# Fetching four consecutive ranks' sums with one indirect transfer in the third layer's node stage

## The reference

```
q, k, v = x @ Wq + bq, x @ Wk + bk, x @ Wv + bv          # 8 heads of 16
e = edge_attr @ We
alpha = softmax over the edges of one node of (q[dst] * (k[src] + e)).sum / 4
agg   = segment_sum(alpha * (v[src] + e), dst)            # 50,000 x 128, zero where a node has no edge
h     = layernorm(agg + x @ Wskip + bskip + x)
x     = layernorm(x + layernorm(gelu(h @ Wf1 + bf1) @ Wf2 + bf2 + h))
```

## Time and profile before

| | |
|---|---|
| Time, median of 3 runs | 7075.83 us (7072.01 to 7086.69) |
| The profiled execution's own time | 7071.4 us |
| Its span, first to last instruction | 7069.7 us |
| Mean granted TensorE clock | 0.883 of full speed |
| Busy over the span: PE, DVE, ACT, POOL | 75%, 59%, 39%, 60% |
| `nodes_2`, from POOL's first fetch to its last scatter | 4332 to 5837 us |
| Busy in 4458 to 5720 us (1262 us): PE, DVE, ACT, POOL | 850.7, 603.9, 655.0, 646.1 us |
| Indirect transfers L435 in the stage | 392, mean 969 ns of POOL |

### The profile page before, as it was taken

One profiled execution on the slowest core, in us unless ns is written; L12 is line 12 of the kernel. 1 busy time (PEld: TensorE's weight loads), 2 busy tenths in 40 slices (PEclk: granted clock), 3 DMA queues, 4 the chain that ended last, 5 costly groups with the idle time before them and its releaser, 6 DMA issues. The chain is left out here.

```text
span 7069.7 us, 108538 instructions
## 1 busy us (share of the span) xinstructions
PE 5276.6 (75%) x29030; PEld 3736.3 (53%) x29030; DVE 4158.6 (59%) x14866; ACT 2748.0 (39%) x6645; POOL 4214.4 (60%) x3907
## 2 busy tenths in 40 slices
PE   4776889788866665787699996766666675776788
PEld 3655677545455554333488874333333344555566
DVE  4454777523345555777488884544445454655698
ACT  0000555411111212666355554555555462222354
POOL 4664466666668886777644442455555445554598
PEclk9898999988888887999799998888888887888899
DMA  4554666444456666999545552333333332333466
GB/s 128 174 173 150 178 179 177 136 124 135 131 117 107 106 108 128 317 301 303 176 141 147 152 148 74 90 86 88 86 89 90 84 87 60 74 72 72 121 185 175
DMA packets 1163875, 966.37 MB, mean 137 GB/s; under 512 B 161046, under 2 KB 975586, under 8 KB 1163268
## 3 DMA queue, kind: packets, MB, share of 16 engines
q1 hardware_dynamic: 977956, 684.36, 32.2%
q0 software_dynamic: 163072, 210.16, 15.4%
q10 hardware_dynamic: 22240, 64.90, 2.5%
HBM read 485.30 MB, written 496.79 MB: 139 GB/s over the span
## 5 line engine op out<-in xcount | busy, mean ns | idle before, releaser
L2337 PE MATMUL l_nodes_f<-l_nodes_h_t_s,w_f 128*128 128x512 f32 x784 | 435.7, 684 | 433.4 <-ACT l_nodes_act_t L2289 422.9
L526 POOL DMA_INDIRECT tgt_tab<-l_nodes_ext,rank_at x392 | 389.9, 995 | 580.9 <-ACT l_nodes_ext L2312 474.0
L1556 POOL DMA_INDIRECT agg<-l_edges_b_rows,l_edges_b_at x392 | 608.5, 1552 | 133.9 <-issue 79.4
L1844 POOL DMA_INDIRECT l_edges_kv<-kv_tab,src_i x392 | 397.7, 1015 | 400.6 <-DVE l_edges_v_e L1865 291.2
L526 POOL DMA_INDIRECT to_col<-l_nodes_col_s,rank_row x392 | 415.4, 1060 | 326.6 <-ACT l_nodes_col_s L1250 232.3
L2510 POOL DMA_INDIRECT l_edges_proj<-proj_tab,src_i x392 | 382.3, 975 | 376.8 <-DVE l_edges_msg L2483 247.7
L435 POOL DMA_INDIRECT l_nodes_ag<-agg,sum_at x392 | 380.0, 969 | 241.4 <-issue 119.5
L961 POOL DMA_INDIRECT l_edges_fetched<-in_x,src_i x392 | 381.5, 973 | 218.8 <-DMA dst_i<-in_dst 111.0
L1314 POOL DMA_INDIRECT l_edges_a_at_row<-to_row,src_i x392 | 378.2, 965 | 219.0 <-issue 111.6
L526 POOL DMA_INDIRECT q_tab<-l_nodes_qkvs,rank_at x392 | 403.0, 1028 | 149.5 <-issue 105.9
L891 ACT COPY l_edges_rows<-l_edges_sums 128x264 f32<-128x264 f32 (+1 forms) x294 | 122.1, 450 | 947.9 <-DMA dst_i<-in_dst 463.7
(11 more groups left out here) (359 smaller groups left out, 14716.8 us busy)
## 6 DMA issues: line engine op xcount, KB each, us to landing
agg<-zeros ACTq DMA_DIRECT2D x98, 516.0 KB
l_nodes_xg<-x SPq DMA_DIRECT2D x196, 256.0 KB
kv_tab<-l_nodes_qkvs SPq DMA_DIRECT2D x98, 512.0 KB
agg<-l_edges_rows SPq DMA_DIRECT2D x98, 266.0 KB
l_nodes_ag<-agg SPq DMA_DIRECT2D x98, 266.0 KB
proj_tab<-l_nodes_ext SPq DMA_DIRECT2D x98, 264.0 KB
l_nodes_ag<-agg SPq DMA_DIRECT2D x98, 258.0 KB
l_nodes_ag_odd<-agg SPq DMA_DIRECT2D x98, 258.0 KB
```

Source lines behind the costliest of these rows:

```text
L526: pool.indirect_dma_start(table, bass.IndirectOffsetOnAxis(ranks[:, n * G + j:n * G + j + 1].bitcast(U32), 0), rows[:, j, :], None, bounds ...
L1556: pool.indirect_dma_start(agg1[j // 2], bass.IndirectOffsetOnAxis(at[k][:, j:j + 1].bitcast(U32), 0), rows[k][:, j, :], None, compute_op=A ...
L1844: pool.indirect_dma_start(kv[k][:, j, :], None, kv_tab, bass.IndirectOffsetOnAxis(src_i[:, n * G + j:n * G + j + 1].bitcast(U32), 0),).the ...
L2337: pe.matmul(f[m % 2][:], w_f1[:, m * P:(m + 1) * P], h_t_s[k][:], start=True, stop=True).then_inc(f_done, 1)
```

## The change

The four transfers of a group become one. It reads, for each partition, a run of four consecutive rows of `agg2` (512 floats, 2 KB) that begins at the lowest of the partition's four row numbers. Since the four nodes' ranks ascend, the row of each of them is one of the four in the run. A node without edges has the row number `held`; it takes nothing from the run, or zeros where `held` lies in it. Marks decide it.

`rank_rows` for the nodes now leaves, in place of `sum_at`, the tile `run_at` (128 x 98, the lowest row number for each partition and group) and `run_mark` (128 x 98 x 4 x 4 floats): mark m, j is 1 where node j's row is row m of the run and 0 elsewhere. Marks with j below m are neither written nor used, since row m of a run can't belong to an earlier node than the m-th.

In `conv` DVE now computes, instead of one addition, `ua[j] = skip[j] + sum over m of ag[m] * mark[m, j]`: 4 + 3 + 2 + 1 = 10 operations on 128 x 128, each a multiplication by a value per partition and an addition. An operation with m above 0 waits through the new semaphore `chosen` for the one that wrote the same part of `ua`.

```diff
-        sum_at, rank_at = (sb0(n, [P, tiles], I32) for n in ("sum_at", "rank_at"))
+        rank_at, run_at = sb0("rank_at", [P, tiles], I32), sb0("run_at", [P, groups], I32)
+        run_mark = sb0("run_mark", [P, groups, G, G])
...
-        def sum_fetcher(space, table, width):
+        def run_fetcher(space, table, width):
...
-            a_in = [[sem(f"a_in{k}{j}") for j in range(G)] for k in range(RING)]
+            a_in = [sem(f"a_in{k}") for k in range(RING)]
...
-                for j in range(G):
-                    pool.indirect_dma_start(
-                        ag[k][:, j, :], None, table, bass.IndirectOffsetOnAxis(sum_at[:, n * G + j:n * G + j + 1].bitcast(U32), 0),
-                    ).then_inc(a_in[k][j], 16)
+                pool.indirect_dma_start(
+                    ag[k][:].rearrange("p j d -> p (j d)"), None, table, bass.IndirectOffsetOnAxis(run_at[:, n:n + 1].bitcast(U32), 0),
+                ).then_inc(a_in[k], 16)
...
-                for j in range(G):
-                    eng.wait_ge(a_in[k][j], i * 16 + 16)
+                eng.wait_ge(a_in[k], i * 16 + 16)
...
-                            for m, (at_p, to) in enumerate(((whole_p, rows), (opens_p, rank_at))):
-                                dve.wait_ge(turned, m + 1)
-                                chain(dve.tensor_copy(to[:].rearrange("p (g j) -> p j g", j=G),
-                                                      at_p[:, 0:tiles].rearrange("p (j g) -> p j g", j=G)))
+                            by_run = "p (j g) -> p g j"
+                            dve.wait_ge(turned, 1)
+                            chain(dve.tensor_copy(sum_f[:], whole_p[:, 0:tiles].rearrange(by_run, j=G)))
+                            chain(dve.tensor_reduce(base[:], sum_f[:], AX.X, ALU.min))
+                            chain(dve.tensor_copy(rows[:], base[:]))
+                            chain(dve.tensor_tensor(sum_f[:], sum_f[:], by_group, ALU.subtract))
+                            for m in range(G):
+                                chain(dve.tensor_scalar(run_mark[:, :, m, m:], sum_f[:, :, m:], float(m), None, ALU.is_equal))
+                            dve.wait_ge(turned, 2)
+                            chain(dve.tensor_copy(rank_at[:].rearrange("p (g j) -> p g j", j=G), opens_p[:, 0:tiles].rearrange(by_run, j=G)))
...
-                            dve.tensor_tensor(ua[k][:], ag[k][:], skip[k][:], ALU.add).then_inc(ua_done, 1)
-                            dve.wait_ge(ua_done, n + 1)
+                            done = n * (G * (G + 1) // 2)
+                            for m in range(G):
+                                for j in range(m, G):
+                                    if m:
+                                        dve.wait_ge(chosen, done - (G - m) + 1)
+                                    so_far = ua[k] if m else skip[k]
+                                    last = dve.scalar_tensor_tensor(ua[k][:, j, :], ag[k][:, m, :], run_mark[:, n, m, j:j + 1], so_far[:, j, :],
+                                                                    ALU.mult, ALU.add).then_inc(chosen, 1)
+                                    done += 1
+                            dve.wait_ge(chosen, done)
+                            dve.sem_inc(ua_done, 1)
                             measure(dve, i, k, A, ua[k])
```

More of the change, by code:

```diff
@@ L658, in rank_rows @@
                 numbers_s = [sb(f"numbers{m}", [groups, GE]) for m in range(2)]
+                sum_f = sb("sum_f", [P, groups, G])
                 with nc.Block() as block:
@@ L2151, in nodes_2 @@
                 measure, chain, wait_ready, factors, apply_norm = norm_pairs(space, "ln", LAGS)
-                ag, fetch, arrived = sum_fetcher(space, agg2, D)
+                ag, fetch, arrived = run_fetcher(space, agg2, D)
                 scatter, scattered, settle, clear_tail, tail_cleared = scatter_steps(space, tgt_tab, rank_at)
@@ L2165, in nodes_2 @@
                     [sem(f"{n}{k}") for k in range(RING)] for n in ("skip_in", "x2_in", "ext_out", "x3_out"))
-                ua_done, a_normed, h_turned, h_copied = (sem(n) for n in ("ua_done", "a_normed", "h_turned", "h_copied"))
+                chosen, ua_done, a_normed, h_turned, h_copied = (sem(n) for n in ("chosen", "ua_done", "a_normed", "h_turned", "h_copied"))
                 f_done, gelu_done, y_done, ub_t_done, b_turned, ub_done = (
@@ L2709, in gnn @@
             with nc.sbuf_tensor("local_node", [P, tiles], F32) as local_node:
-                rank_rows("node_ranks", has, local_node, node_base, node_line, rows=sum_at, present=rank_row)
+                rank_rows("node_ranks", has, local_node, node_base, node_line, rows=run_at, present=rank_row)
         nodes_0()
```

## The result

The changed kernel takes 6623.88 us (median of 4 runs, 6621.27 to 6625.67), the kernel before beside it 7073.92 us (4 runs, 7068.26 to 7086.69). The ratio is 0.936, 95% interval 0.935 to 0.937: 450 us faster. The forecast was 6698 us in a range of 6600 to 6930 us.

The account below looks back on a forecast made before the run. Late increments from POOL's long unbroken transfer runs were taken to bound `nodes_2`. Terms: -365 (middle) - 15 (start) + 3 (`rank_rows`) = -377 us from 7071.4, 6694, plus 4.4 to the median: 6698 us; own range 6620 to 6840, 8-in-10 range 6600 to 6930.

Parts of the forecast that it names:

- What bounds the kernel: Middle of `nodes_2`: some 6 us of each 15.2 us round are waits, with semaphore increments late during POOL's long transfer runs.
- POOL: In `nodes_2`, eight transfers a round become five, 6.4 us of work, fetch 1.0 us, about 3 us of pause each round.
- DVE: In `nodes_2`, ten operations take 2.9 us, one of 0.7 us goes: 2.2 us more a round, bounds 1.9 and 3.1 us.
- The round: Middle of `nodes_2`: 10.8 us a round instead of 15.2, bounds 9.9 and 12.5; 365 us less over 83 rounds.
- the pair of 20.6 us: Two `nodes_2` rounds, 11.4 us with `chain` and 9.2 us without; 0.6 us clock loss and 0.4 us late increments make 21.6.
- Ends of the stage: First 63 us and last 75 us of `nodes_2` keep their length, at worst 9 us more, apart from 15 us saved early.
- The fill: Start of `nodes_2`: ten fetches take POOL 13 us instead of 50 us; 15 us less, bounds 0 and 25 us.
- `rank_rows`: Eight DVE operations come and one goes between two barriers, uncovered: 3 us more, at least 1 and at most 6.3 us.
- A: In `nodes_2`, increments stay late in part, 2.6 us a round left: rounds of 13.4 us, time 6914 us; chance 12%.
- B: Nothing changes: a 2 KB row costs POOL 3.8 us as before, or moved bytes cause lateness; 7070 to 7080 us; chance 4%.
- C: Slower: POOL's runs and lateness stay and catch `conv`'s new waits, 196 us more, 7270 us; chance 5%.
- D: DVE's ten operations wait out POOL's instructions in `nodes_2`, 2.2 us a round, time 6880 us; chance 2%.

Follow-up runs that it names:

- `pieces4`: The kernel after with its fetch split into four transfers of one row each, eight transfers a round: 6088.59 us, ratio 1.005 to the kernel before on chip 1.
- `one_add`: The kernel after with one addition in place of the ten operations, without marks (sums not the nodes'): 5935.25 us, ratio 0.980 to the kernel before on chip 1.
- `pieces3`: The kernel after with its fetch split into three transfers (two rows, one, one): 6066.68 us, ratio 1.002 to the kernel before on chip 1.
- `late_turn`: The kernel after with PE's transposes back moved behind the first half of `widen`, ACT's `copy_b` behind `apply_a`: 5988.23 us, ratio 0.988 to before on chip 10.
- `before_again`: The kernel before, unchanged, run on chip 10: 6056.15 us, ratio 1.000 to the kernel before there.
- `after_again`: The kernel after, unchanged, run on chip 10: 6043.15 us, ratio 0.997 to the kernel before there.

## Why the prediction was right, and where not

- *What bounds the kernel.* That the 6 us a round are a wait that comes with the transfers, and not work, was right on the first chip: all of it went when a round had five transfers, as did the foreign releasers and the late increments (238 of 647 before, 0 of 716 after). The rule behind it, that increments come late "while POOL has long been issuing indirect transfers without a pause", was too wide in two ways. On chips 1, 5 and 10 eight transfers a round, without a pause, delay nothing; one chip's trace couldn't tell that. And on the first chip `edges_1b` issues without a pause for a whole stage with nothing late, while `edges_2` has late increments in runs of four; the trace of the kernel before did hold that. What the prediction leaned on for its own stage, that most lateness falls behind the fifth transfer of a run, stands in the table of places, where none of the 112 at places one to four is late. So five being short enough here was read from the right rows, but it was in part luck that this stage has no stricter limit. That the number of transfers and not another part of the change (such as rows of 2 KB, or the slower rounds) ended the lateness is not shown on a chip of the first kind: `pieces4` and `one_add` never met one.
- *POOL.* Five transfers and 3 us of pause: right. The fetch was put at 1.0 us; in the middle it took 1.16 us on average, within the bounds of 0.97 to 1.55, and it is hidden.
- *DVE.* 2.9 us for the ten, 2.96 measured; rounds of 11.4 and 9.2 us, 11.3 and 9.2 measured.
- *The round.* The mis-sized term is what was added to the pair of 20.6 us: 0.6 us for the clock and 0.4 us for late increments, a guess. Measured are 20.68 us a pair, so both together are about 0.1 us. Three of the rounds of 9.2 us became 10.9 us, and the clock stayed at 0.99. The row behind the clock's price shows less than was read: the granted clock was still 1.00 over the idle time of 2.35 us (5046.58 to 5048.94) and 0.69 over the four products behind it, so it was not at its lower level when they began. That makes 10.34 us a round and not 10.8, 38 us. The other 12 us of the middle are before's own round, 15.34 us by the starts and 15.2 us by counting groups in a window.
- *Ends of the stage.* The fill gave 20 us, 15 expected. The first rounds cost 10 us; I had them at nothing and named 9 us as the worst. From the third distance on they are 10.5 to 11.3 us, as in the middle; DVE's idle time lies before the first three results (16.6 us of waits for PE's `y` there), and covers nothing behind them.
- *`rank_rows`.* 3 us expected. From the second L742 copy to the next stage's first L499 it was 8.3 us and is 10.6 us: 2.3 us.
- *Not seen.* 25 us in `nodes_3`. Of the 74 us by which the time is below the forecast they are the part that the prediction had no term for, and so luck in its favour; 50 us are the middle of `nodes_2`. The time of 6624 us is 4 us above the lower end of the forecast's own range.
- *The rivals.* A (late increments stay in part) is refuted on the first chip: a run of four scatters and a fetch holds nothing back. B and C rest on POOL still writing four transfers' worth for a row of 2 KB; it doesn't. Nor do the moved bytes make the lateness, B's other case: they are the same, and it went. What C describes, waits of `conv` caught while lateness stays, was not tried on a chip that has it. D (DVE waits for POOL) is refuted in its direction: L2223 takes 344 to 348 ns beside POOL, L2257 348 ns. It is POOL that pays: the unchanged scatter's transfer went from 997 to 1171 ns on the first chip, and 992 ns in `one_add` stand against 1106 ns in `pieces4` on chip 1. POOL's pauses hide it, save in `pieces4` and perhaps `pieces3`. The Trainium skill's page "SBUF — State Buffer", section "SBUF: two separate sides", says that a VectorE operation with two inputs in SBUF and a GpSimd operation that reads SBUF take turns on shared ports; the trace agrees for POOL's side alone (997 to 1171 ns), not for DVE's (344 to 348 ns).

## What to carry to other kernels

When waits end long after the work they wait for, beside an engine that issues indirect transfers without a pause, first take the kernel before to another chip: here the same program takes 6057 or 7074 us, and the change is worth 0.3% or 6.4%. Then test the rule that you read from one stage on the other stages of the same trace: here two of them, `edges_1b` and `edges_2`, already spoke against "long and without a pause". A change that takes transfers off a full POOL and puts work on DVE pays only if DVE's new work is not on the path; here its ten operations made every second round 2 us longer, and only when PE's transpose was moved away from DVE's last result could the other rounds, 1 us shorter then, make up for part of it. Compare stages and not only totals: 24 us of this change's gain lie in a stage that it doesn't touch.

## What was not expected of the hardware

- Chips of one kind differ by 15 to 17% on this kernel (6057 us on 1, 5 and 10; 6957 us on 11; 7074 us on the first), at nearly equal durations of POOL's transfers (997 and 1012 ns for L526), by when waits end.
- The late increments are mostly PE's, some DVE's and none ACT's (238 of 647, 125 of 1345, 0 of 937 in the middle of before on the first chip).
- DVE's multiply-adds with two tensors from SBUF made POOL's transfers longer to issue: L526 went from 997 to 1171 ns on the first chip, from 1012 to 1071 ns on chip 10 (1182 ns in `late_turn`).
- A predicated copy of 128 x 384 floats takes 0.59 us, of 128 x 128 0.29 us.
- In `nodes_3` DVE's small operations on 128 x 8 take 0.17 us, and some about 0.5 us. All 143 of before's 750 that take over 0.3 us have a TENSOR_SCALAR of POOL starting in their time or up to 0.3 us before it; so do 142 of the 607 others. Which operations are hit differs between before and after (L304 and L296 in `before_again`, L298 and L310 in `after_again`).
